# Key and query products in three fp16 passes, roots by a ScalarE guess, and a new order of work

## The reference, cut to what matters

```python
for i in range(DEPTH):                       # 6 layers
    xn = _layernorm(x, ln1_w[i], ln1_b[i])   # (x - m) * rsqrt(v + 1e-5) * w + b
    q, k, v = xn @ wq[i], xn @ wk[i], xn @ wv[i]       # split into 8 heads of 16
    q = softmax(q, over the 16 of a head); k = softmax(k, over the 1024 rows)
    context = einsum('bhnd,bhne->bhde', k, v)
    x = einsum('bhnd,bhde->bhne', q, context) @ wo[i] + bo[i] + x
    xn = _layernorm(x, ln2_w[i], ln2_b[i])
    hdn = xn @ w1[i]; hdn = where(hdn >= 0, hdn, 0.01 * hdn)
    x = hdn @ w2[i] + x
...
x = x0 + gate_a * x; h = layernorm(x) * (1 + cb) + sb
out = x + gate_b * fp4_linear(silu(fp4_linear(h, w_gate)) * fp4_linear(h, w_up), w_down)
```

## Time and profile before

| what | value |
|---|---|
| median of three runs | 1198.66 us (1196.38 to 1200.05) |
| span of the profiled execution, first to last instruction | 1196.8 us |
| median less span | 1.9 us |
| instructions | 28581 |
| mean granted TensorE clock, share of full speed | 0.984 |

### The profile page before, as it was taken

One profiled execution on the slowest core, in us unless ns is written; L12 is line 12 of the kernel. 1 busy time (PEld: TensorE's weight loads), 2 busy tenths in 40 slices (PEclk: granted clock), 3 DMA queues, 4 the chain that ended last, 5 costly groups with the idle time before them and its releaser, 6 DMA issues.

```text
span 1196.8 us, 28581 instructions
## 1 busy us (share of the span) xinstructions
PE 1129.7 (94%) x9722; PEld 864.8 (72%) x9722; DVE 1074.1 (90%) x2885; ACT 1035.2 (86%) x1776; POOL 1090.7 (91%) x920
## 2 busy tenths in 40 slices
PE   7787999999999999999999999999999888999996
PEld 5574687787777777777778778777777755565664
DVE  7889889999999999999999999999987479999973
ACT  5687999999999999999999999999998795767753
POOL 4888999999999999999999999999999888999762
PEclk8799999999999999999999999999999999999998
DMA  8121778768778777687777776866767420110000
GB/s 308 36 71 53 214 213 217 188 209 219 179 205 217 194 216 189 193 221 177 219 212 182 224 202 190 220 194 194 214 188 217 107 61 21 44 37 36 19 19 36
DMA packets 213857, 190.13 MB, mean 159 GB/s; under 512 B 113392, under 2 KB 192080, under 8 KB 213712
## 3 DMA queue, kind: packets, MB, share of 16 engines
q1 hardware_dynamic: 213712, 188.31, 56.3%
HBM read 87.06 MB, written 76.02 MB: 136 GB/s over the span
## 4 chain that ended last, share of the span: by engine, by line
POOL 34%; PE 27%; issue 22%; DVE 10%; ACT 3%; DMA 2%; SPq 2%; DVEq 0%; POOLq 0%; ACTq 0%
POOL hidden L1787 15%; POOL rows_split L1779 6%; POOL arena L1760 4%; POOL arena L1793 3%; PE pair_mlp L576 2%; PE pair_mlp L556 2%; PE ring_pair L615 2%; PE ring_pair L616 2%; PE ring_pair L617 2%; PE pair L567 2%; PE pair L599 2%; DVE ring_pair L1371 2%; DVE arena L1508 2%; PE pair_mlp L674 1%; DVE arena L1389 1%
## 5 line engine op out<-in xcount | busy, mean ns | idle before, releaser
L1787 POOL TENSOR_TENSOR hidden<-hidden 128x2048 f16<-128x2048 f32 x92 | 376.1, 4088 | 0.0
L883 ACT ACTIVATE hidden<-ring_pair,hidden_bias 128x512 f32<-128x512 f32 x384 | 245.6, 686 | 27.9 <-PE ring_pair L617 27.5
L892 ACT ACTIVATE hidden<-hidden 128x2048 f16<-128x2048 f32 x96 | 183.4, 1911 | 17.8 <-PE mlp L633 15.6
L1100 DVE BATCH_NORM_STATS2 bn<-x_all 128x6 f32<-128x128 f32 x896 | 184.2, 278 | 3.2 <-POOL x_all L1739 1.9
L1713 POOL TENSOR_TENSOR rstd<-ve,minus_half 128x8 f32<-128x8 f32 x104 | 170.5, 1640 | 0.0
L852 ACT ACTIVATE arena<-x_all,nmr,rstd 128x128 f32<-128x128 f32 x384 | 157.9, 495 | 0.0
L615 PE MATMUL ring_pair<-arena,halves 128*128 128x512 f16 x384 | 146.1, 381 | 4.5 <-DMA arena<-rows_split 2.8
L616 PE MATMUL ring_pair<-arena,halves 128*128 128x512 f16 x384 | 146.0, 380 | 0.0
L617 PE MATMUL ring_pair<-arena,halves 128*128 128x512 f16 x384 | 145.9, 380 | 0.0
L631 PE MATMUL mlp<-halves,hidden 128*128 128x128 f16 x768 | 135.9, 219 | 1.4 <-POOL hidden L1787 1.4
L633 PE MATMUL pair_mlp<-halves,hidden 128*128 128x128 f16 x768 | 136.5, 220 | 0.0
(11 more groups left out here) (206 smaller groups left out, 3145.1 us busy)
## 6 DMA issues: line engine op xcount, KB each, us to landing
n_away<-all_blocks SPq DMA_DIRECT2D x47, 512.0 KB, 3.3
norm_raw<-n_away SPq DMA_DIRECT2D x188, 128.0 KB, 3.0
k_away<-all_blocks SPq DMA_DIRECT2D x45, 512.0 KB, 2.8
q_away<-all_blocks SPq DMA_DIRECT2D x45, 512.0 KB, 3.3
arena<-k_away SPq DMA_DIRECT2D x180, 128.0 KB, 3.6
arena<-q_away SPq DMA_DIRECT2D x180, 128.0 KB, 3.6
x_all<-in_L_attn_x SPq DMA_DIRECT2D x8, 512.0 KB, 5.4
x_in<-in_L_attn_x SPq DMA_DIRECT2D x8, 512.0 KB, 4.0
```

The source lines that it names most:

```text
L883: act.activation(hidden_t[:, c * W + h * HALF:c * W + (h + 1) * HALF], ring[n % 2], ACT.Prelu, bias=hidden_bias[:, b:b + 1], scale=HIDDEN_ ...
L892: act.activation(half_rows(hidden_hi, h), half_rows(hidden_t, h), ACT.Copy).then_inc(hidden_hi_ready, 1)
L1100: last = nc.vector.bn_stats(bn[:, 6 * t:6 * t + 6], src(t))
L1787: pool.tensor_tensor(half_rows(hidden_lo, h), half_rows(hidden_t, h), half_rows(hidden_hi, h), ALU.subtract).then_inc(hidden_lo_ready, 1)
```

## The change

Key and query products are made of three fp16 products each, like the MLP's. For that the rows after the first norm are copied to a high fp16 half by ScalarE (`first_norm_high`, in the place of `first_norm_t`) and a low one by GpSimd (`first_norm_low`, new). The first norm's weight and bias are folded into `wq` and `wk` once, at the start: GpSimd builds a 128x128 matrix for each layer, TensorE multiplies, VectorE bounds the results, and a scale, a power of two, is found, spread and applied (`fold_products` to `qk_low`). The scale is undone inside the two exponentials (`scale=qk_ups[...]`), and for the keys' maximum by a new 128x1 step (`scale_k`). SyncE no longer loads `wk` and `wq` by layer, but all at once at the start.

The two `pow` calls of an item become one sequence of small steps for both norms at once, on 128x16 numbers: ScalarE takes `exp(-0.5 * ln(v + eps))` as a guess, GpSimd does one Newton step (`root_open` to `root_raise`, 8 instructions). A joint sequence `r` serves the first norm of item `r` and the second of item `r - 4`.

Every engine's list is in a new order, with an item spread over more iterations (VectorE: `add_mlp(v - 7, 0)` and `add_mlp(v - 8, 1)` instead of v - 6 and v - 7), the first item goes through DRAM too (`FIRST_N` 0), and `keep_warm` is gone.

```diff
-    FIRST_N, FIRST = 1, 3
+    FIRST_N, FIRST = 0, 3
...
+            def fold_products():                                   # TensorE
+                pe.wait_ge(qk_loaded, 2 * 16)
+                pe.wait_ge(fold_rows_ready, DEPTH)
+                for bank, raw in ((S0, wq_raw), (S1, wk_raw)):
+                    for l in range(DEPTH):
+                        last = nc.tensor.matmul(tile(bank, l), tile(fold_rows, l), tile(raw, l), start=True, stop=True)
...
             def product_k(i):
...
-                    last = nc.tensor.matmul(S1[:, h * HALF:(h + 1) * HALF], w, norm1_t..., start=True, stop=True)
+                    nc.tensor.matmul(o, hi, rows_hi, start=True, stop=False)
+                    nc.tensor.matmul(o, lo, rows_hi, start=False, stop=False)
+                    last = nc.tensor.matmul(o, hi, rows_lo, start=False, stop=True)
...
             def product_q(i):
...
-                    last = nc.tensor.matmul(tile(S0, t), tile(norm1_t, t), w, start=True, stop=True)
+                    nc.tensor.matmul(tile(S0, t), tile(norm1_hi, t), hi, start=True, stop=False)
+                    nc.tensor.matmul(tile(S0, t), tile(norm1_hi, t), lo, start=False, stop=False)
+                    last = nc.tensor.matmul(tile(S0, t), tile(norm1_lo, t), hi, start=False, stop=True)
...
+            act.preload_act_table_set("natural_log_exp_and_others")
...
+            def root_guess(v):                                     # ScalarE
+                after(act, mv1_ready, min(v + 1, ITEMS))
+                after(act, mv2_ready, min(v - LAG + 1, ITEMS))
+                after(act, root_steps, rooted(v - 1, SQUARED))
+                act.activation(root_log[:, :], mv[:, :, 1], ACT.Ln, bias=eps_cols[:, 0:1]).then_inc(root_log_ready, 1)
+                act.wait_ge(root_log_ready, v + 1)
+                act.activation(root_y[:, :], root_log[:, :], ACT.Exp, scale=-0.5).then_inc(root_y_ready, 1)
...
+            def qk_low(l):                                         # VectorE
+                dve.wait_ge(qk_hi_ready, DEPTH)
+                for to, hi, bank, c in ((wq_lo, wq_hi, S0, l), (wk_lo, wk_hi, S1, DEPTH + l)):
...
-            def root1(j):                                          # GpSimd
...
-                root(rstd1, ve1, T, j + 1, pow1_done)
...
+            def root_square(v):
+                pool.wait_ge(root_y_ready, v + 1)
+                pool.tensor_tensor(root_a[:, :], root_y[:, :], root_y[:, :], ALU.mult).then_inc(root_steps, 1)
...
+            def first_norm_low(i):
+                pool.wait_ge(norm1_hi_ready, i + 1)
+                after(pool, q_done, i)
+                pool.tensor_tensor(norm1_lo..., norm1_raw..., norm1_hi..., ALU.subtract).then_inc(norm1_lo_ready, 1)
```

832 lines of the change are left out of this document (465 added, 367 removed).

## The result

The changed kernel takes 1228.31 us (four executions, 1224.72 to 1232.41), the one before 1197.52 beside it: a ratio of 1.0243 [1.0208, 1.0278]. It is slower; 1180 (1160 to 1210) was forecast. The profiled execution took 1227.89 us, its span is 1226.1, 29.3 more than the 1196.8 of before.

The account below looks back on a forecast made before the run. No single engine explained the time; TensorE asked most per item, 18.4 us. From a span of 1196.8, - 19 + 14 - 16 + 2 = 1177.8; with 1.9 between span and median, 1180 us, range 1160 to 1210.

Parts of the forecast that it names:

- The beat: Time per item in the middle: falls from 18.44 to 18.0 us (17.6 to 18.6), -19 us over 43 items.
- The root handover: Rival: GpSimd and ScalarE wait for each other at the root; beat up to 19.0, 1223 us; chance 0.15.
- a table load in the loop: Rival: ScalarE loads activation tables twice an item, 131 us over 51 sequences, 1311 us; chance 0.02.
- a beat at 18.4: Rival: GpSimd's bounds or a narrow 0.5 us place keep the time per item at 18.4; 1199 us; chance 0.13.
- a draining at 18.2 a beat: Rival: the last four items still take 18.2 us each, with no gain there; 1196 us; chance 0.12.
- The start: Span start to item 0's mark: first key product at 56, 17 us late; +14 us (+5 to +25).
- The draining: Last four beats, item 43's mark to item 47's: 57 us against 72.8, -16 us (-22 to 0).
- Mark to network: Item 47's mark to the feed-forward unit called `x_rows(6)`: 31 to 33 us against 29.7, +2 us (-1 to +6).
- 176.7 carried over: From that feed-forward unit to the end of the span: VectorE's list unchanged, so 176.7 us stays.
- The clock: Start without `keep_warm`: lower clock free where VectorE is waited for, at most 7 us where products are on the path.
- the sentence on the Trainium skill: Start: by the skill's clock-gate rule alone, removing the filler costs 7 us more and the sum is 1187.

Follow-up runs that it names:

- bias_early: Changed kernel with `hidden_bias_cols` moved back ahead of `output_bias_rows` on TensorE; 1210.12 us, 1.0069 of the kernel before.
- after_again: The changed kernel itself, unedited, timed and profiled a second time; 1217.09 us, 1.0142 of the kernel before.
- both: Changed kernel with `hidden_bias_cols` ahead of `output_bias_rows` and the lists from iteration 50 written out in nearly the old order; executions 1202.21, 1221.49, 1220.37, 1226.97 us.
- both_again: The same kernel as both, timed again in twelve executions; median 1202.26 us, 1.0043 of the kernel before.
- no_weight_lows: The kernel of both, with VectorE's twelve MLP-weight low halves made for 8 of 512 columns and two GpSimd `memset` added; 1199.7 us, 1.0008 of the kernel before.
- steady_start: The kernel of both, with `round_weights` and `prepare_gates` behind `block_n`, `block_n(0)` ahead of `weight_bounds(1)`, `first_norm_low(0)` ahead of `front_rows(3)`; 1228.64 us, 1.0241.
- tail_order: Changed kernel with lists from iteration 50 written out, the network's first units beside the same item steps as before the change; 1211.94 us, 1.0083.
- warm: Changed kernel with 220 filler products put on TensorE in the start, the first 60 ahead of `hidden_bias_cols`; 1223.48 us, 1.0196 of the kernel before.

## Why the prediction was wrong, point by point

- **The beat: right.** 18.0 forecast, 17.95 to 17.97 measured where nothing is held. Each price held: `product_k` 1.30 (1.29), `product_q` 1.34 (1.34), the low half 2.16 (2.16), the eight small steps 0.20 to 0.22 each and the guess 0.32 and 0.22 (0.29 and 0.19). ScalarE became the bound, at 98.8 to 99.8%, with TensorE at 97 outside one window. The held instruction took 7.8 of the 21 us; no step foresaw it.
- **The root handover, the rival of the other side: fell.** The result is near its 1223, by other causes. Its signs did not come: in the whole run GpSimd is idle 0.4 us ahead of `root_square`, and ScalarE 0.0 ahead of `normalise2`. What the guess itself waits for is VectorE's `mv`, 17.0 us in all: 7.78 behind the held instruction and 4.93 in the start, so 4.3 us over the other fifty. Nor was there a table load in the loop. The rivals of a beat at 18.4 and a draining at 18.2 a beat did not come to pass either.
- **The start (+14, its bound +25): the failed step, +33.8** (+29.3 in the second profile). It failed in two terms. The first is a wait left out: the step walked VectorE's and GpSimd's lists up to 56, and of TensorE's only the fold, while `hidden_bias_cols` had moved behind a product that waits 12.5 us. That is +6 to +11 (bias_early), 3.1 us of it the clock. The second is VectorE's new work, put at 10 us. Up to item 0's mark VectorE's busy and idle time are:

| kernel | mark 0 | VectorE busy | VectorE idle |
|---|---|---|---|
| before | 124.5 | 106.8 | 17.8 |
| after | 158.3 | 126.9 | 31.4 |
| after_again | 153.8 | 127.3 | 26.6 |
| bias_early | 147.6 | 126.9 | 20.8 |
| both | 145.5 | 127.4 | 18.2 |
| both_again | 143.9 | 123.4 | 20.5 |

With the line moved back, the idle time is within 3 us of the old one, and what is left of the start (19.4 to 23.1 us) is VectorE's longer busy time, 16.7 to 20.6 us more and not 10. In the run both, counted by instructions, which overlap a little, some 13 of it are new ones, 5 are one more batch's statistics and two more transposes that fall ahead of the mark, and 7 are the twelve low halves, which take longer than before. That reads like VectorE's load as the cause, but it stays open: no run took the load out cleanly (no_weight_lows held the start up elsewhere), and a longer chain through the front rows would look alike. The first item's way in is not it: 7.0 us off it moved the mark by 0.5 (steady_start).
- **The draining (-16): the right sign, mis-sized.** It gave -4.9, and only because the network's first units no longer shared it: in the old order it is +2.3 (tail_order). The idle 8.7 us of the earlier trace rows were read as a gap that a longer spread would close. From 960 on there was little gap left to close: VectorE was busy 34.70 of 40 us with the network's first units among its work.
- **Mark to network (+2): failed in two ways.** The unit was misnumbered, and the step counted VectorE's 20 us of put-off work as fitting in the same 30 us. TensorE's gate product runs 35 us later; the term was +13.3. Draining and this term belong together: -4.9 + 13.3 = +8.4 against -14 forecast.
- **176.7 carried over: held**, 177.5, and 176.5 in two other runs.
- **The clock: right in kind, other products.** The granted clock did fall: 0.59 in 80 to 100 us, mostly the level of 1.2 GHz, where 0.87 stood before. The prediction had it cost nothing where VectorE is waited for, and at most 7 us where products on the path take longer. The products on the path were the 48 of `hidden_bias_cols`, 10.24 us at the low level and 7.12 partly at the high one: 3.1 us, where the whole stretch ran at the low level. Behind the first key product no price is seen (warm). Of the 7 us that the sentence on the Trainium skill (TensorE: Matmul & The Clock Gate, Part 1: The HAM clock gate) gave to the filler's removal, these 3 are there; in the kernel before, taking the filler out made the mark 1.4 and 4.5 us earlier.

## What to carry to other kernels

When a change brings new lists for all engines, walk each engine's list, TensorE's too, for instructions that crossed a wait; one line that had crossed one cost 6 to 11 us here, up to half of what the shorter beat won. Work that fills the gaps of a draining phase must be counted as part of it: a draining that gets shorter while its filler is put off has gained nothing. And when a run takes work out or puts filler in to test a cause, read its trace for what the edit itself put on the chain: here two `memset` held the start up by 4.5 us and hid most of what the removed work gave, and 60 fillers hid what the clock gave.

## What the runs showed of the hardware

- **A VectorE instruction held for 8 us.** Four were seen in three profiles (9.76, 9.45, 9.44, 9.46 us, each a 1.1 to 1.5 us instruction), and none of that length in the others. Each stood behind the same `small` step, started while GpSimd ran its large instructions without a gap, four or more from there on, and ended 0.3 to 0.6 us behind the last of them. The executions of one kernel differ in such amounts: 1198.4 to 1200.8 and then 1207.5 and 1207.8 in no_weight_lows. That those slower ones hold such an instruction wasn't profiled, and is only argued. Three of the four have one SBUF input, so the port rule cited above, taken by its two-input condition alone, would not have pointed at them; no view here shows whether they ran in a 2-port mode.
- **A `memset` holds VectorE too.** Two of GpSimd's, 5.25 us together, held a VectorE instruction of 0.22 us for 5.26 (no_weight_lows against both_again). Here the edit added the `memset`, so the cause is shown, and the instruction has one SBUF input and 128 columns.
- **Smaller instructions save less than their size beside GpSimd.** The same eight columns cost 0.16 us in one place and 1.5 in another; 512 columns cost 1.3 and 2.0 in these two. Over all twelve, 64 times fewer columns left 57% of the time (10.6 of 18.4 us).
- **A clock that falls can be free, or not.** Leaving 172 fillers out won 0.3% in two comparisons. The same low level cost 3.1 us where 48 products stood on the chain.
- **One kernel, two occasions.** The changed kernel stood at 1.0243 and at 1.0142 of the one before. The two profiles are 10.4 us apart: 4.5 in the start and 6.6 in the 43 beats, where the held instruction cost 7.8, with -0.6 behind them. The other executions were not profiled.
